# Moving the gating products of a Mamba-2 mixer from VectorE to GpSimd

## The reference, cut to what matters

```
h = layernorm(x) * (1 + ca) + sa
z, xBC, dt = split(h @ W_in.T)                  # 1024, 1280, 16 columns
xBC = silu(conv4(xBC) + b_conv)                 # x (1024), B (128), C (128)
Y = Y_diag + Y_off                              # the state-space scan, 16 heads of 64
y = Y + Dp * X
y = y * silu(z)                                 # the gate
y = y * rsqrt(mean(y * y) + 1e-5) * norm_w
x = x + ga * (y @ W_out.T)
x = x + gb * ffn(layernorm(x) * (1 + cb) + sb)
```

## Time and profile before

| what | value |
|---|---|
| median of three runs | 1644.73 us |
| the profiled execution | 1644.31 us |
| span of that execution, first to last instruction | 1642.6 us |
| TensorE busy | 1511.9 us (92%) |
| VectorE busy | 1197.8 us (73%) |
| ScalarE busy | 623.1 us (38%) |
| GpSimd busy | 303.0 us (18%) |
| mean granted TensorE clock | 0.976 of full |

### The profile page before, as it was taken

One profiled execution on the slowest core, in us unless ns is written; L12 is line 12 of the kernel. 1 busy time (PEld: TensorE's weight loads), 2 busy tenths in 40 slices (PEclk: granted clock), 3 DMA queues, 4 the chain that ended last, 5 costly groups with the idle time before them and its releaser, 6 DMA issues. The chain is left out here.

```text
span 1642.6 us, 26879 instructions
## 1 busy us (share of the span) xinstructions
PE 1511.9 (92%) x8289; PEld 1233.0 (75%) x8289; DVE 1197.8 (73%) x2556; ACT 623.1 (38%) x1208; POOL 303.0 (18%) x344
## 2 busy tenths in 40 slices
PE   4989999989999999999999999765999999999998
PEld 4977777877777777877777777544888888888887
DVE  3689998988988988988988988734554554643632
ACT  3346456455544554554554564311121111211210
POOL 1302212311221221221121122121111111111011
PEclk9799999999999999999999999887999999999999
DMA  7322222222222222122122221117012022021110
GB/s 253 110 89 78 80 76 78 72 84 77 71 83 77 71 83 77 51 99 81 40 88 69 75 77 65 65 55 259 14 64 78 7 70 69 7 77 44 33 52 27
DMA packets 61377, 124.25 MB, mean 76 GB/s; under 512 B 13296, under 2 KB 15984, under 8 KB 56816
## 3 DMA queue, kind: packets, MB, share of 16 engines
q1 hardware_dynamic: 55632, 114.68, 20.0%
q10 hardware_dynamic: 5664, 8.65, 1.5%
HBM read 97.62 MB, written 25.69 MB: 75 GB/s over the span
## 5 line engine op out<-in xcount | busy, mean ns | idle before, releaser
L805 DVE SCALAR_TENSOR_TENSOR xBC<-conv_in,wconv,xBC 128x256 f32<-128x256 f32 x480 | 231.3, 485 | 12.8 <-ACT xBC L602 1.4
L1399 ACT ACTIVATE silu_gate<-bank,sgate 128x512 f32<-128x512 f32 x88 | 60.6, 688 | 384.1 <-PE bank L1518 384.1
L1453 DVE SCALAR_TENSOR_TENSOR hidden<-bank,sup,silu_gate 128x512 f32<-128x512 f32 x88 | 66.1, 751 | 146.3 <-PE bank L1518 146.3
L601 ACT ACTIVATE conv_in<-bank 128x256 f32<-128x256 f32 x160 | 61.4, 384 | 243.2 <-PE bank L1087 243.2
L1172 PEld LDWEIGHTS bank<-X,decay 128*128 128x128 f32 x1024 | 122.4, 194 | 29.0 <-issue 21.4
L1518 PE MATMUL bank<-ff_h_high,W_gate 128*128 128x512 f32 x352 | 141.5, 402 | 2.4 <-DVE ff_h_low L1441 2.4
L1518 PE MATMUL bank<-ff_h_low,W_gate 128*128 128x512 f32 x352 | 140.1, 398 | 0.0
L1518 PE MATMUL bank<-ff_h_high,W_up 128*128 128x512 f32 x352 | 139.6, 397 | 0.0
L1550 PE MATMUL bank<-W_down,hidden_high 128*128 128x512 f32 x352 | 139.5, 396 | 0.0
L1550 PE MATMUL bank<-W_down,hidden_low 128*128 128x512 f32 x352 | 139.5, 396 | 0.0
L1518 PE MATMUL bank<-ff_h_low,W_up 128*128 128x512 f32 x352 | 139.4, 396 | 0.0
(11 more groups left out here) (170 smaller groups left out, 3288.2 us busy)
## 6 DMA issues: line engine op xcount, KB each, us to landing
decay<-sums_scratch SPq DMA_DIRECT2D x32, 1024.0 KB, 4.8
wq_rows<-wqT SPq DMA_DIRECT2D x33, 256.0 KB, 3.9
widened_scratch<-wq_rows SPq DMA_DIRECT2D x33, 256.0 KB, 2.1
x_tile<-x SPq DMA_DIRECT2D x32, 256.0 KB, 2.8
x_resid<-x SPq DMA_DIRECT2D x32, 256.0 KB, 2.7
x_scratch<-x_resid SPq DMA_DIRECT2D x32, 256.0 KB, 2.0
ff_x_tile<-x_scratch SPq DMA_DIRECT2D x32, 256.0 KB, 3.3
ff_x_resid<-x_scratch SPq DMA_DIRECT2D x32, 256.0 KB, 4.0
```

The lines of the kernel that those rows point to most:

```text
L601: nc.scalar.activation(A.raw[:, m, 3:3 + SC], ps[:, 0:SC], ACT.Copy)
L805: nc.vector.scalar_tensor_tensor(A.xc[b][:, m, :], A.raw[:, m, j:j + SC], A.wconv[:, m, j:j + 1], A.xc[b][:, m, :], ALU.mult, ALU.add).the ...
L1399: nc.scalar.activation(B.sg[m % 2][:], gates[m % 2][:], ACT.Silu, scale=T.sgate[:, m:m + 1]) \
L1453: nc.vector.scalar_tensor_tensor(B.hid[m % 2][:], ups[m % 2][:], T.sup[:, m:m + 1], B.sg[m % 2][:], ALU.mult, ALU.mult).then_inc(hid_step, 1)
```

## The change

The function `gate` moves from VectorE's program to GpSimd's. It does the same three operations on the same tiles with the same waits for its inputs, and signals `gated` as before. The semaphore `gate_z` and VectorE's waits for it go. On GpSimd `gate(n, u, b, 0)` stands between `times_D(n, u, 0)` and `inv_rms(n, u, 0)`, and `gate(n, u, b, 1)` between `residual(n, u, b, 0)` and `inv_rms(n, u, 1)`.

```diff
@@ block.gpsimd @@
+            def gate(n, u, b, c):
+
+                wait(pool, yoff_read, u, 2 * NC, 2 * c + 2)
+                wait(pool, ydiag_read, u, 2 * NC, 2 * c + 2)
+                nc.gpsimd.tensor_tensor(A.yt[:], A.yt[:], A.XD[:], ALU.add).then_inc(y_summed, 1)
+                wait(pool, y_summed, u, NC, c + 1)
+
+                a_wait(pool, a_emptied, u, ("z", 2 * c + 1), 1)
+                nc.gpsimd.tensor_tensor(A.yt[:, 0:Z], A.yt[:, 0:Z], A.siluz[:, c, :], ALU.mult)
+                wait(pool, siluq_done, u, 1, 1)
+                nc.gpsimd.tensor_tensor(A.yt[:, Z:], A.yt[:, Z:], A.zdt[1 - b][:, c, 0:ZQ], ALU.mult).then_inc(gated, 1)
+
...
                 if bef:
                     times_D(n, u, 0)
+                    gate(n, u, b, 0)
                     inv_rms(n, u, 0)
                     times_D(n, u, 1)
                 if nxt:
                     rstd(after(n))
                 if bef:
                     residual(n, u, b, 0)
+                    gate(n, u, b, 1)
                     inv_rms(n, u, 1)
                     residual(n, u, b, 1)
...
@@ block.vector @@
-            def gate(n, u, b, c):
-
-                wait(dve, yoff_read, u, 2 * NC, 2 * c + 2)
-                wait(dve, ydiag_read, u, 2 * NC, 2 * c + 2)
-                nc.vector.tensor_tensor(A.yt[:], A.yt[:], A.XD[:], ALU.add).then_inc(y_summed, 1)
-                wait(dve, y_summed, u, NC, c + 1)
-
-                a_wait(dve, a_emptied, u, ("z", 2 * c + 1), 1)
-                nc.vector.tensor_tensor(A.yt[:, 0:Z], A.yt[:, 0:Z], A.siluz[:, c, :], ALU.mult).then_inc(gate_z, 1)
-                wait(dve, siluq_done, u, 1, 1)
-                nc.vector.tensor_tensor(A.yt[:, Z:], A.yt[:, Z:], A.zdt[1 - b][:, c, 0:ZQ], ALU.mult).then_inc(gated, 1)
-                wait(dve, gate_z, u, NC, c + 1)
-
...
                 if bef:
-                    gate(n, u, b, 0)
                     read_state(u, b, 0, 0)
...
                     decay_X(n, u, 1)
-                    gate(n, u, b, 1)
                 if nxt:
                     norm(after(n), n, 0)
```

More of the change, by code:

```diff
@@ L359, in mixer_stage @@
         yoff_read, ydiag_read, S_step = sem("yoff_read"), sem("ydiag_read"), sem("S_step")
-        rstd_step, XD_done, y_summed, gate_z, gated, rs_step, out_step = (
-            sem(s) for s in ("rstd_step", "XD_done", "y_summed", "gate_z", "gated", "rs_step", "out_step"))
+        rstd_step, XD_done, y_summed, gated, rs_step, out_step = (
+            sem(s) for s in ("rstd_step", "XD_done", "y_summed", "gated", "rs_step", "out_step"))
         accs, tps = A.psum[0:2], A.psum[2:4]
```

## The result

The changed kernel takes 1731.56 us (median of 4 runs, 1730.76 to 1743.05), beside 1645.51 us before. The ratio is 1.0547 (95% interval 1.0519 to 1.0576): 86 us slower. The prediction was slower, 1695 us with a range of 1640 to 1745. Its direction and its first mechanism were right, and its third rival, the clock, came true on top. The profiled execution has a span of 1740.9 us; over 19 runs of the changed kernel the span went from 1728.1 us at a mean clock of 0.947 to 1741.3 us at 0.939.

A forecast was written before the change was run, and what follows sets the result against it. TensorE and VectorE were taken as nearly full, with VectorE's state reads setting TensorE's pace. 15 turns x (1.57 + 1.83) = 51 us on 1644.3 gave 1695 us, own range 1655 to 1725, stated range 1640 to 1745.

The forecast's parts named there:

- first mechanism: On VectorE after `decay_X`: GpSimd's gate products block `conv` and `norm`, so state reads come 1.57 and 1.83 us later.
- third rival: On TensorE: longer waits for the state read halve the clock for 4 us each, 60 us more, 1755 us; chance 0.11.
- Removal: On VectorE: two gates a turn leave, 2.55 us each; at most TensorE's 44.9 us of state-read waits go.
- GpSimd's durations: A gate on GpSimd takes 4.90 us: 2.35 us for 1024 columns, 1.81 for 768, 0.74 for 256.
- Exclusion: GpSimd and VectorE products with all operands in SBUF do not overlap; `norm` counted as blocked; 0.13 us saved per handover.
- The sum of the block: Turns 1 to 15: state reads later by 1.57 us in tile 0 and 1.83 us in tile 1, 51 us together.
- with TensorE's busy time in it unchanged: Sign in the mixer's turn: it becomes 67.9 us long instead of 64.5, while TensorE is busy as long as before.
- Sharing: First rival: GpSimd and VectorE share instead of excluding each other, 44.9 us of waits are gained, 1599 us; chance 0.14.
- Cancelling: Second rival: only GpSimd's add blocks VectorE, about 2.5 us a gate, and the effects cancel at 1644 us; chance 0.05.
- The last turn: Turn 16, with no convolution beside its gates: counted as nothing, with 5 us either way for its two tiles.

The follow-up runs named there:

- the run with one-tensor operations and constant scalars: The changed kernel with GpSimd's three gate products replaced by operations on one tensor (y times 1 plus a constant, same columns): 1608.13 us, ratio 0.9774.
- the differences with scalars from SBUF: The kernel before, gate on VectorE, with tile 1's 16 differences (line 875) moved from VectorE to GpSimd: 1644.95 us, ratio 1.0002.
- the run with the clock held: The changed kernel with 12 throwaway 128x128 matmuls on TensorE ahead of each wait for the first state read: 1691.34 us, ratio 1.0274.
- In another order: The kernel before with both gates on VectorE moved behind the first state read of their tile: 1659.78 us, ratio 1.0093.

## Why the prediction was right, and where it was short

- **Removal.** The prediction said that no more than 44.9 us could be gained at this place. Without any gate the kernel gained 54 us: the waits, and 8.3 us of TensorE's busy time that went with them. It counted a wait at its own length, and a wait costs somewhat more.
- **GpSimd's durations.** Behind the handovers 2.22, 1.68 and 0.61 us were predicted. The add ends 2.24 us behind `decay_X`, the 768 columns 1.69 us behind the first `conv` step and the 256 columns 0.58 us behind the second. In the last turn, with no `conv` beside them, the 768 and 256 columns take 1.81 and 0.72 us, where 1.81 and 0.74 were worked out. Dividing the 512-column product into a fixed part and 2.10 ns a column was the right reading.
- **Exclusion.** Right in kind and place: `conv` and `norm` stand still while GpSimd's product runs, as in rows 9 and as the Trainium skill says (SBUF — State Buffer, section "SBUF: two separate sides"). The run with one-tensor operations and constant scalars agrees with it too. Only the differences with scalars from SBUF depart from that page, which lets any GpSimd operation that reads SBUF hold the ports for its whole length: beside them `conv` kept its 1.52 us, and in rows 10 it was 1.71.
- **The sum of the block.** 15 x 3.40 = 51 us was predicted. The rows after give 15 x (1.36 + 1.63) = 45 us, and the run with the clock held gives 45.9. In its trace the state reads fall 2.8 us further behind in each turn from 2 to 15, and 5.6 us in the first with a gate, so the close match owes a little to luck.
- **The clock.** This is the term that was missing. "Both TensorE waits grow, from about 1.5 to about 3.2 us" was right (3.08 us here, 2.9 on average), and the sum then took the slower clock behind them as nothing and gave the third rival 0.11. It came true on top of the block, for 40 us where that rival had 60. The sign "with TensorE's busy time in it unchanged" failed: busy time went from 1511.9 to 1569.5 us. From turn 2 to 14 a turn takes 63.3 us before, 66.2 with the clock held (2.8 more, where 3.4 was forecast) and 69.7 in the changed kernel. Rows 13 showed what a wait of 5.09 us does and rows 4 what 1.72 us does; 3.1 us turned out to lie on the bad side. The spread of the 19 runs has the same look, longer spans at a lower clock.
- **The range.** The forecast's own range was 1655 to 1725 us, and 1731.56 lies outside it. It is inside the stated 1640 to 1745 only because the upper end had been moved two thirds of the way to the clock rival. The direction and the block were worked out; that the number fell inside is owed to the widening.
- **The rivals.** Sharing was wrong for the gate's products. Rows 10, on which it rested, are of a form that does leave VectorE free, but not because it reads one tile. Cancelling was wrong.
- **The last turn** was left at nothing, within 5 us. With the clock held, the first state read of tile 1 is 45.1 us behind the kernel before in turn 15 and 46.4 us in turn 16, so it adds about 1.3 us.

## What to carry to other kernels

An idle GpSimd is not free room for VectorE's float32 products of two SBUF tiles: each runs about twice as long there, and VectorE's `conv` and `norm` stood still for all of it. When a variant with other operations is faster, compare where each instruction ends on both engines before naming the reason: here the shorter operations excluded VectorE just as the long ones did. Before moving work off an engine, look at what stands between it and whoever waits for it, since reordering the same instructions gave 1.3% where moving them lost 5.5%. When a change makes TensorE wait longer, price the clock as well as the wait; throwaway matmuls that end inside the wait tell the two apart, and in this kernel took back 40 of 86 us.

## What the runs showed of the hardware

- Two waits of 3.0 us a turn brought the mean granted clock of the mixer from 1.00 to 0.94, and 2.8 us of throwaway matmuls in each brought it back to 1.00. In another order, two waits of 0.79 and 0.94 us, 3.5 us apart, were followed by a window at 0.70. Waits of 1.26 and 1.72 us 29 us apart left it at 1.00.
- VectorE's `conv` and `norm` steps that found a GpSimd product at work ended 0.28 us behind it, in both tiles of the turn shown. Behind GpSimd's one-tensor operations with constant scalars it was 0.27 us.
- GpSimd's one-tensor operation with constant scalars took 0.83 and 0.40 us alone for 768 and 256 columns. With scalars read from SBUF, 128 columns took 0.81 us on average (13.01 us for 16), and VectorE's `conv` beside it 1.52 us for three steps, as if alone.
- A 128x128 float32 matmul by the identity, one after the other, took 0.23 us each (5.08 us for 22) at a full clock. The profile counts each as two.
